# Attention stage of a scan, expert and attention kernel: transposes and norm statistics moved between steps

## The reference, cut to what matters

```python
x = x + attention(_layernorm(x))              # the stage that is changed
x = x + experts(_layernorm(x))                # its first quad is normed and turned during attention

q, k, v = x @ Wq.T + bq, x @ Wk.T + bk, x @ Wv.T + bv    # 16 query heads, 4 key/value heads of 32
q, k = rope(q), rope(k)
att = where(causal, q @ k.T / sqrt(32), -inf)             # 512 x 512 for each head
y = softmax(att) @ v
return y @ Wo.T + bo
logits = x @ gate_w.T                                     # expert layer: the router
```

## Time and profile before

| | us |
|---|---|
| median of 3 runs (3074.55 to 3083.29) | 3078.28 |
| the profiled execution | 3065.87 |
| its span, first to last instruction | 3064.1 |
| PE busy in the span | 2744.9 (90%) |
| DVE, ACT, POOL busy | 1780.0, 1298.1, 1527.1 |
| attention, first score to next stage's first matmul | 1602.0 to 2250.3 |
| granted TensorE clock, mean of the span | 0.945 |

### The profile page before, as it was taken

One profiled execution on the slowest core, in us unless ns is written; L12 is line 12 of the kernel. 1 busy time (PEld: TensorE's weight loads), 2 busy tenths in 40 slices (PEclk: granted clock), 3 DMA queues, 4 the chain that ended last, 5 costly groups with the idle time before them and its releaser, 6 DMA issues.

```text
span 3064.1 us, 37572 instructions
## 1 busy us (share of the span) xinstructions
PE 2744.9 (90%) x13484; PEld 1444.4 (47%) x13484; DVE 1780.0 (58%) x3787; ACT 1298.1 (42%) x2689; POOL 1527.1 (50%) x944
## 2 busy tenths in 40 slices
PE   4668889898997989988868999999899999999998
PEld 2455555555555534433335555555444444444443
DVE  5899999999999742222236666665624444222222
ACT  4557576675765401110017666666721221111111
POOL 5999999999999612212126555555500001121211
PEclk7769999999999989989989999999999999999999
DMA  5444554545545479999950000000225323899997
GB/s 191 143 167 152 195 172 161 194 153 195 172 161 183 164 263 348 344 341 338 335 173 1 29 29 29 29 28 15 89 86 181 119 88 129 310 337 341 340 348 211
DMA packets 198955, 557.76 MB, mean 182 GB/s; under 512 B 24880, under 2 KB 26800, under 8 KB 198256
## 3 DMA queue, kind: packets, MB, share of 16 engines
q1 hardware_dynamic: 180624, 513.27, 48.5%
q0 software_dynamic: 17088, 40.90, 5.8%
q10 hardware_dynamic: 1056, 1.18, 0.1%
HBM read 479.50 MB, written 75.79 MB: 181 GB/s over the span
## 4 chain that ended last, share of the span: by engine, by line
PE 52%; DVE 4%; ACT 3%; POOL 2%; issue 2%; DMA 1%; POOLq 0%; SPq 0%; DVEq 0%; ACTq 0%
PE bank L1128 11%; PE bank L1154 5%; PE bank L1031 5%; PE bank L1052 5%; PE bank L1066 5%; PE bank L1179 4%; PE bank L1236 3%; PE bank L1213 3%; PE bank L1201 2%; ACT arena L1758 2%; POOL arena L1935 2%; PE bank L1225 1%; PE bank L1111 1%; DVE arena L1546 1%; PE bank L1167 1%
## 5 line engine op out<-in xcount | busy, mean ns | idle before, releaser
L1839 POOL TENSOR_TENSOR arena<-arena 128x1024 f32<-128x1024 f32 x256 | 605.9, 2367 | 6.0 <-PE bank L981 2.9
L1687 ACT ACTIVATE bank<-arena 128x512 f32<-128x512 f32 x512 | 346.5, 689 | 312.8 <-DVE arena L1325 194.2
L1935 POOL TENSOR_TENSOR arena<-arena 128x2048 f32<-128x2048 f32 (+3 forms) x128 | 296.7, 2321 | 286.5 <-DVE arena L1555 286.5
L981 PE MATMUL bank<-arena 128*128 128x128 f32 x2048 | 305.2, 302 | 143.7 <-POOL arena L1845 143.3
L981 PEld LDWEIGHTS bank<-arena 128*128 128x128 f32 x2048 | 259.3, 156 | 230.1 <-POOL arena L1845 184.4
L1758 ACT ACTIVATE arena<-arena 128x256 f32<-128x256 f32 (+3 forms) x512 | 286.0, 561 | 187.9 <-DVE arena L1546 157.4
L1128 PE MATMUL bank<-arena 128*64 128x352 f32 x2048 | 343.0, 491 | 0.0
L1845 POOL TENSOR_TENSOR arena<-arena 128x512 f32<-128x512 f32 x256 | 333.7, 1304 | 16.1 <-DVE arena L1325 16.1
L1325 DVE TENSOR_TENSOR_SCAN arena<-bank,arena 128x512 f32<-128x512 f32 x256 | 310.8, 1214 | 24.8 <-POOL arena L1839 18.6
L1325 DVE TENSOR_TENSOR_SCAN bank<-bank,arena 128x512 f32<-128x512 f32 x256 | 308.5, 1205 | 0.0
L1903 POOL DMA_INDIRECT arena<-scratch_xn,arena x64 | 68.6, 1071 | 460.9 <-DVE arena L1514 231.6
(11 more groups left out here) (145 smaller groups left out, 4159.1 us busy)
## 6 DMA issues: line engine op xcount, KB each, us to landing
arena<-scratch_bc SPq DMA_DIRECT2D x128, 1024.0 KB, 5.4
arena<-in_w_gate SPq DMA_DIRECT2D x128, 704.0 KB
arena<-in_w_up SPq DMA_DIRECT2D x128, 704.0 KB
arena<-in_w_down SPq DMA_DIRECT2D x128, 512.0 KB
arena<-in_w_down SPq DMA_DIRECT2D x128, 192.0 KB
scratch_x<-arena SPq DMA_DIRECT2D x16, 1024.0 KB, 4.5
scratch_xn<-arena SPq DMA_DIRECT2D x15, 1024.0 KB, 4.1
arena<-scratch_x SPq DMA_DIRECT2D x44, 256.0 KB, 6.0
```

The source lines that it names most:

```text
L981: i = nc.tensor.matmul(y[:, t * P:(t + 1) * P], w[:, n, t * P:(t + 1) * P], p.ident, is_transpose=True, start=False, stop=g == GROUPS - 1 ...
L1687: nc.scalar.activation(bank[p.da_bank(k, n)][:, :], block_of(p.dt, b, c), ACT.Exp, scale=p.alog[:, c, state:state + 1]).then_inc(*p.decaye ...
L1839: nc.gpsimd.tensor_tensor(out=p.hb[k % HB], in0=over(block_of(p.dtx, b, c), 1, NG), in1=p.bc[k // 2 % NBC][:, 0], op=ALU.mult).then_inc(*p ...
L1935: nc.gpsimd.tensor_tensor(out=own, in0=own, in1=over(p.rden[:, k % 2, :], 2, width), op=ALU.mult).then_inc(*p.divided.up(k))
```

## The change

Four edits, all in the list of work:

1. In steps with a `turn`, the turns now stand right behind `score`, ahead of `weigh` and the flips; their copies `turned` now stand in the same step, ahead of its four exponentials. Before, the turns were last in their step and the copies ahead of the next step's exponentials.
2. The norm of the batch after next is earlier: the first half of `stats` at s7 and the rest at s8 (all at s9 before), `rstd` at s9 (s10), `apply` at s11 (s12). `bias` stays at s13 and s15.
3. The `stats` of F(1,0) are in two pieces, at s2 and s3 of the last batch (all at s3 before). Its `rstd` and `apply` stay at s4 and s6.
4. The four turns of F(1,0) go from the tail to s10, s11, s12 and s13 of the last batch, and its `gate_wide` and `gate` from the end of the tail to its first two steps.

No instruction is added to PE, ACT, POOL or SP. `stats_a` and `stats` issue the same four row tiles as before.

```diff
@@ batch_steps @@
     if b + 2 < BATCH:
         if b > 0:
             add(2, [("xa_in", b + 2)])
-        add(9, [("stats", then)])
-        add(10, [("rstd", then)])
-        add(12, [("apply", then)])
+        add(7, [("stats_a", then)])
+        add(8, [("stats", then)])
+        add(9, [("rstd", then)])
+        add(11, [("apply", then)])
...
     if b == BATCH - 1:
         add(1, [("ff_w", m)])
+        add(2, [("stats_a", early)])
         add(3, [("stats", early)])
         add(4, [("rstd", early)])
         add(6, [("apply", early), ("xn_out", m, q)])
+        for c in range(HC):
+            add(10 + c, [("turn", early, c)], [("turned", early, c)])
     if b == BATCH:
-        for c in range(HC):
-            add(c, [("turn", early, c)], [("turned", early, c)])
-        add(5, [("gate_wide", m, q)], [("wide_out", m, q)])
-        add(6, [("gate", m, q)], [("logit", m, q)])
+        add(0, [("gate_wide", m, q)], [("wide_out", m, q)])
+        add(1, [("gate", m, q)], [("logit", m, q)])
@@ attention_plan @@
         plan += pending
         weighs = [m // QT - 1] if m > 0 and m % QT == 0 and m <= nsteps else []
-        plan += [("weigh", n) for n in weighs] + [("pflip", *f) for f in flips]
+        makes, pending = beside[k % (REP * QT)]
+        turns, turned = [i for i in makes if i[0] == "turn"], [i for i in pending if i[0] == "turned"]
+        plan += turns + [("weigh", n) for n in weighs] + [("pflip", *f) for f in flips]
+        plan += turned
...
-        makes, pending = beside[k % (REP * QT)]
-        plan += makes
+        plan += [i for i in makes if i not in turns]
+        pending = [i for i in pending if i not in turned]
```

## The result

| | before | changed |
|---|---|---|
| median of the first comparison, us | 3071.65 (10 runs) | 3058.69 (10 runs) |
| ratio of the runs, 95% interval | | 0.995, 0.9934 to 0.9966 |
| the profiled execution's span, us | 3064.1 | 3057.4 |
| attention, first score to next stage's first matmul | 648.28 | 634.82 |
| ahead of attention | 1602.01 | 1608.78 |

The change is faster by 13.0 us; I had forecast 10.8 and a time of 3067.5, so the time is under my range (3060.5 to 3074.5). The interval leaves out 1; its middle, 0.995, is not the ratio of the two medians, which is 0.9958. The spans differ by only 6.7 us because the stages ahead of attention, in which nothing was changed, took 6.8 us longer in this one execution. Read from attention's own start, the gain is 13.46.

The account below looks back on a forecast made before the run. Batches 1 to 6 were taken as PE-bound but for some 1.5 us each, with real pauses at both ends. Terms 7.8 + 1.2 + 1.2 + 0.6 = 10.8 us off 3078.3 gave 3067.5 us, range 3060.5 to 3074.5.

Parts of the forecast that it names:

- Batches 1 to 6: PE's waits at s0 to s2 shrink with earlier turns and ACT starting sooner: 1.30 us a batch, 7.8 in all.
- the wait for POOL at s15: Sign named for the norm's earlier step: exponentials of s15 wait some 0.4 us less for POOL.
- Batch 0: Split, earlier statistics let the score of s11 start 2.7 us sooner and the projection 1.2 us sooner; ends 0 and 2.9.
- as it is: Batch 0's projection, 5.27 us where 3.70 is usual, at half clock for a while, was left unchanged.
- Batch 7 to s10: Half of F(1,0)'s statistics at s2 brings the score of s5 1.2 us sooner; ends 0 and 2.8.
- The tail: Moved turns and gates let the next stage start at 2249.7 and not 2250.29: 0.6 us, ends -1.5 and 1.5.
- the tail's first product 1.35 later: Cost of putting turns and copies into s10 to s13, where ACT has little spare time: 1.35 us.
- I keep: The 1.7 us that half clock cost the tail's first weigh (4.06 against 2.36) was assumed to stay.
- I carry the difference over: The profiled execution is 12.4 us below the runs' median; this was kept, so 3078.3 - 10.8 = 3067.5 us.
- The wait only changes its place: Rival, 25%: ACT stays full; batches give 5.2, whole 8.2 (3070.1 us); far end 5.4 in all, 3072.9 us.
- The half clock at the ends goes: Rival, 14%: shorter pauses in batch 0 and before s5 of batch 7 keep the clock up; 14.1 us, 3064.2.
- The clock falls in every batch: Rival, 5%: PE's pauses at s0 to s2 become four small ones and lower the clock; slower, 3087.9 us.

Follow-up runs that it names:

- first comparison: The changed kernel, all four edits, against the kernel before: medians 3058.69 us (10 runs) and 3071.65 (10 runs), ratio 0.995.
- edit 4: Kernel before with only F(1,0)'s turns at s10 to s13, last in their steps, and gates at the tail's start: batch 7 with the tail 99.04 us.
- the first profile of before: Profile of the unchanged kernel before: attention 648.28 us, batch 0 68.05, tail 36.20.
- the second profile of before: The kernel before profiled again, no edit: attention 646.60 us, batch 0 66.97, tail 34.50.
- filler: Repeated PE transposes in a pause: seven repeats in batch 0 of the kernel before, 65.69 us; six in batch 7 of the changed kernel, 96.11 us.
- the second comparison: The changed kernel again, no edit, against the kernel before: medians 3059.56 us (7 runs) and 3069.36 (12 runs), ratio 0.9959.
- edit 1 alone: Kernel before with only turns first in their step and their copies ahead of that step's exponentials: batches 1 to 6 take 79.04 us each.

## Why the prediction was right or wrong

**Batches 1 to 6: right.** 8.0 us against 7.8, split as it said: 0.93 from the turns, 0.41 from the norm's step. What was wrong is small: the wait before the weigh was 0.33 and not 0.55, and the wait for POOL at s15 did not get shorter, it only came sooner.

**Batch 0: 2.81 against 1.2, and the term was mis-sized twice.** The steps were right (the score of s11 waits 0.30, then flips wait for ACT, 1.17 and 0.32). From the score of s10 to the end of the batch the changed kernel takes 26.7 us and before, at full clock, 27.4 (4.86 + 22.50): structure is worth 0.7 and not 1.2, so these flips waited longer than I had it. The 1.7 behind it, which I left "as it is", are the half clock. The last 0.4 stand ahead of s10 (39.00 us before, 38.56 changed), a stretch in which the score of s8 takes 1.9 to 2.1 us and not 1.14 in all fourteen profiles; it is 38.15 to 39.02 long, so this is a difference of executions as well.

**Batch 7 to s10: 1.13 against 1.2.** Right, with the clock still low behind it in this profile. It also fell less often after the shorter wait.

**The tail: 1.46 against 0.6, inside its ends only by accident.** The term was a sum of "the tail's first product 1.35 later" and the savings behind it. With the turns first in their steps it is 2.16 later (17.48 to 19.64; the 1.35 is what edit 4 gives alone), so the structure loses 0.2 us. The gain shown is the 1.7 of the weigh at half clock in the first profile of before, which "I keep": it is no property of the kernel, since the second profile of before doesn't have it.

So the structure gives 0.7 + 8.0 + 1.2 - 0.2 = 9.7, and the other 3.8 of the 13.46 is the difference between two executions in where the clock was low. Over many executions a part of that is probably real, since the clock fell less often after the shorter pauses in batch 0 and before s5. From the table, without the runs with a filler there: s5 to s10 takes 28.15 in the mean of six behind the longer pause, and 26.55 in six behind the shorter, 1.6 less; behind the score of s11 the clock cost 1.3 in the mean of five and nothing in eight; the tail's mean loss is 0.4 either way. 9.7 + 1.6 + 1.3 = 12.6 is what I would now forecast, an estimate from six to eight profiles of several kernels. By medians the two comparisons gave 13.0 and 9.8; as ratios their intervals are 10.4 to 20.3 and 7.1 to 18.1 us, and both hold it.

**The level: the step that put the time out of the range.** The text says of the 12.4 us between the profiled execution and the median "I carry the difference over". That median was one of three runs. With seven more runs beside them the median of the same kernel is 3071.65 (10 runs), and in the second comparison 3069.36 (12 runs). Of the 8.8 us by which 3067.5 was high, this step made 6.6 and the effect 2.2. From 3071.65 the forecast of 10.8 would have given 3060.9, within the range; with the effect forecast exactly (13.0) the step would still have given 3065.3, 6.6 high. The table shows where this spread lives: attention starts between 1602.0 and 1618.9, behind attention all take 813.4 to 813.9. Why the stages ahead of attention differ by up to 17 us stays open.

**Rivals.** "The wait only changes its place" fell: 2.0 us of new waits before the weighs stand against the 5.8 that went, and edit 1 alone gave 79.04. (Its far end was also added wrongly: 0.4 a batch off 8.2 leaves 5.8, not 5.4.) "The half clock at the ends goes" gave 14.1 and 3064.2, closest to what one pair of profiles shows, but its reason (shorter pauses) holds for batch 0 and in part for s5, not for the tail. "The clock falls in every batch" fell: 1.00 in batches 1 to 6. But its premise did not come either: the three pauses of a batch became two (0.26 and 0.33) and not four, so the changed kernel did not put it to the test. The Trainium skill (TensorE: Matmul & The Clock Gate, section "HAM oscillation — how this bites in real kernels") shows a loop whose waits put the clock down each time around; here the same wait of 2.41 us did so in some executions only.

## What to carry to other kernels

Before a half-clock stretch behind a pause is entered in a sum, as kept or as gone, take a second profile of the same kernel: here such stretches held 5.7 us of the first profile of before, nearly half of the effect under study: 2.4 in batch 0 (68.05 against 65.69 with the filler), 1.6 from s5 to s10 (27.35 against 25.71 in the changed kernel) and 1.7 in the tail (36.20 against 34.50). A time that is forecast from three runs must allow for the error of their median, and an effect of 10 us in 3000 is read from a stretch with fixed ends, not from the whole. Taking a product ahead in its step paid here where the consumer's queue was full (batches 1 to 6, 0.93 us each), and cost where a long product behind it waited for its bank (s10 of the last batch, 0.57 us, of which 0.26 is the wait).

## What was unexpected of the hardware

- The same PE program with the same pause ran on at 2.4 or at 1.2 GHz from execution to execution: a weigh took 2.36 or 4.05 us after a wait of 2.41.
- A repeat of 18 or 21 transposes in a pause cost nothing measurable: batch 7 took 96.11 us with it and 96.11 without it at the same clock, and batch 0 from the score of s11 on 22.50 and 22.49.
- Undisturbed stretches repeat closely: batches 1 to 6 within 0.03 us over both profiles of the changed kernel and over the five of kernels with these batches as before, and 813.4 to 813.9 us for the whole last stage, while the stages ahead vary by 17.
